# A transformer kernel's opening reordered on all engines: rope of the first half inside the second LayerNorm, keys of two heads loaded first, scores begun on half the tokens

## The reference, cut to what matters

```python
x = L0_attn_x
mod = (_silu(L0_c) @ L0_wmod).reshape(L0_c.shape[0], 6, 1, -1)
h = _layernorm(x, axis=-1) * (1 + ca) + sa
...
q = (x @ Wq.T).reshape(b, t, H, DH).transpose(0, 2, 1, 3)      # H=32, DH=16
k = (x @ Wk.T).reshape(b, t, HKV, DH).transpose(0, 2, 1, 3)    # HKV=8, G=H//HKV=4
v = (x @ Wv.T).reshape(b, t, HKV, DH).transpose(0, 2, 1, 3)
q = q * cos + _rotate_half(q) * sin
k = k * cos + _rotate_half(k) * sin
scores = jnp.einsum('bhgtd,bhkd->bhgtk', qg, k) / math.sqrt(DH)
scores = jnp.where(causal[None, None, None], scores, jnp.finfo(jnp.float32).min)
attn = jax.nn.softmax(scores, axis=-1)
ctx = jnp.einsum('bhgtk,bhkd->bhgtd', attn, v)
```

## Time and profile before

| what | value |
|---|---|
| time, median of 3 runs | 879.16 us (876.94 to 880.44) |
| the profiled execution's own time | 878.1 us |
| its span, from first to last instruction | 876.3 us |
| PE busy | 755.4 us (86%) |
| DVE busy | 521.5 us (60%) |
| ACT busy | 323.4 us (37%) |
| POOL busy | 252.7 us (29%) |
| mean granted TensorE clock | 0.93 of full speed |
| first score matmul of head 0 | at 75.42 us |
| row maxima of head 0 (`nm`) | at 108.11 us |
| first transposed unit of head 0 | at 118.64 us |

### The profile page before, as it was taken

How to read it: one execution, slowest core, us unless ns; L and a number is a source line. 1 busy time by engine, 2 the same in 40 slices (tenths; PEclk the granted TensorE clock), 3 DMA queues, 4 the chain that set the end, 5 groups by cost and what they waited for, 6 DMA issues and landing times.

```text
span 876.3 us, 11777 instructions
## 1 busy us (share of the span) xinstructions
PE 755.4 (86%) x4006; PEld 483.0 (55%) x4006; DVE 521.5 (60%) x761; ACT 323.4 (37%) x544; POOL 252.7 (29%) x190
## 2 busy tenths in 40 slices
PE   2785699999999999879799999677777799998998
PEld 1663243333333433217668888555546678886786
DVE  7733886766767677306845547898798433335410
ACT  3130035665656556661325400334412332322200
POOL 5533733200000000151236532364523122212500
PEclk9795679999999999999999999978698899999999
DMA  8084765610110100211013200110041011111111
GB/s 321 1 163 54 162 140 125 99 62 1 60 61 0 61 28 34 88 37 60 1 49 96 72 1 1 66 37 0 1 75 61 0 62 37 45 48 49 61 60 37
DMA packets 24139, 52.91 MB, mean 60 GB/s; under 512 B 3841, under 2 KB 9833, under 8 KB 22953
## 3 DMA queue, kind: packets, MB, share of 16 engines
q1 hardware_dynamic: 24105, 52.46, 22.7%
HBM read 45.63 MB, written 6.62 MB: 60 GB/s over the span
## 4 chain that ended last, share of the span: by engine, by line
PE 67%; DVE 16%; issue 5%; POOL 4%; ACT 3%; DMA 3%; SPq 1%; ACTq 0%; DVEq 0%; POOLq 0%
PE ps L830 65%; DVE mxp L1655 3%; DVE xnb L1557 1%; ACT pr L1372 1%; DVE arena L1566 1%; PE ps L847 1%; DMA wm<-in_wm 1%; DVE arena L1569 1%; DMA Qst<-q_parts 1%; DMA q_parts<-parts 1%; DVE rt L1850 1%; PE ps L992 1%; DVE st L1539 1%; POOL arena L2056 1%; SPq L702 1%
## 5 line engine op out<-in xcount | busy, mean ns | idle before, releaser
L830 PE MATMUL ps<-arena 128*128 128x512 f32 (+1 forms) x1728 | 429.3, 410 | 37.8 <-DVE arena L1569 15.1
L830 PEld LDWEIGHTS ps<-arena 128*128 128x128 f32 (+1 forms) x1728 | 336.9, 197 | 120.3 <-issue 29.0
L1655 DVE TENSOR_REDUCE mxp<-ps 128x2 f32<-128x1024 f32 (+3 forms) x160 | 173.4, 1116 | 86.4 <-PE ps L830 85.7
L1372 ACT ACTIVATE pr<-ps 128x512 f32<-128x512 f32 x288 | 161.7, 596 | 128.4 <-PE ps L830 125.9
L830 PE MATMUL ps<-Kst,Qst 96*128 (+4 forms) x384 | 107.3, 352 | 21.0 <-DMA Qst<-q_parts 13.8
L830 PE MATMUL ps<-Qst,Kst 99*128 (+1 forms) x288 | 104.7, 385 | 7.5 <-ACT pr L1372 4.3
L830 PEld LDWEIGHTS ps<-Kst,Qst 96*128 (+1 forms) x384 | 37.1, 103 | 88.4 <-issue 48.5
L830 PE MATMUL ps<-maskb,identb 128*128 128x128 bf16 (+1 forms) x320 | 77.7, 264 | 0.0
L830 PE MATMUL ps<-pr,vr 128*32 128x512 f32 x576 | 76.7, 605 | 0.7 <-ACT pr L1372 0.7
L830 PEld LDWEIGHTS ps<-Qst,Kst 99*128 (+1 forms) x288 | 27.2, 97 | 76.3 <-ACT pr L1372 50.0
L2104 POOL COPY vr<-vtok 128x128 f32 (+1 forms) x8 | 2.3, 293 | 204.1 <-PE ps L830 204.1
(11 more groups left out here) (180 smaller groups left out, 735.7 us busy)
## 6 DMA issues: line engine op xcount, KB each, us to landing
wmr<-in_wmr SPq DMA_DIRECT2D x8, 1280.0 KB, 5.5
raw<-in_w SPq DMA_DIRECT2D x16, 512.0 KB, 3.3
Qst<-q_parts SPq DMA_DIRECT2D x18, 256.0 KB, 8.8
q_parts<-qparts SPq DMA_DIRECT2D x3, 768.0 KB, 8.4
x<-in_x SPq DMA_DIRECT2D x8, 256.0 KB, 6.1
wm<-in_wm SPq DMA_DIRECT2D x1, 2048.0 KB, 8.7
raw<-in_up SPq DMA_DIRECT2D x8, 256.0 KB, 2.6
raw<-in_down SPq DMA_DIRECT2D x8, 256.0 KB, 2.6
```

What stands on the lines that cost most here:

```text
L830: return nc.tensor.matmul(outp, lhs, rhs, start=start, stop=stop, skip_group_check=True)
L1372: A(pr[:, k % PRING, :], ps[:, 4 + k % 2, :], ACT.Exp, scale=float(DH) ** -0.5).then_inc(exp_done, 1)
L1655: V.tensor_reduce(mxp[:, kh, g0:g0 + heads, i].rearrange("p (b e) -> p b e", e=per), units, AXX, ALU.max)\
```

## The change

The line numbers of the changed file differ; the names are the same.

- SP: `wm0` comes in four DMAs, one for each of its chunks, with a semaphore each; the second half of x is loaded ahead of the query weights; cosine and sine are loaded by halves. Jobs 0 and 1 are both stored before anything is read back. Of the keys only heads 0 and 1 are read back for each half (`load_keys(0, 2, ...)`), and the keys of heads 2 to 7 after all of them, for the whole length (`k_rest`). Each half has semaphores of its own.
- ACT: writes the three rows of ones of `Kst` (POOL did), splits the key and value weights between the chunks of the first LayerNorm, and takes the first part of job 0 between chunks 1 and 2 of the second.
- POOL: no memset of `Kst`; `wkv_lo` between its two low parts of half 0; the second `rstd` ahead of both `wq_lo_`; sines of jobs 0 and 1 and the last part of job 0 around and inside the second half's low parts.
- DVE: rope of job 0 ahead of the second half's split; job 1's rope and job 0's rest between chunks 1 and 2 of that split (`first_queries`); jobs 2 and 3 afterwards.
- PE: `values(0)` ahead of `queries(0, 0)`; `queries(2, 0)` ahead of the scores; the scores begin once the first half's stacks are in; `queries(2, 1)`, the turning of the values and the wait for the second half's stacks stand ahead of unit 6 (`LATER`); `queries(3, 0)` and `(3, 1)` move from behind units 3 and 6 to behind units 9 and 13. `swap_queries` on DVE moves with them: ahead of unit 6, behind unit 9, behind unit 19.

```diff
-            sp.dma_start(wm0[:, :, :].rearrange("p c n -> p (c n)"), a["wm0"]).then_inc(wm0_in, 16)
+            for kc in range(KC):
+                sp.dma_start(wm0[:, kc, :], a["wm0"][:, 1024 * kc:1024 * (kc + 1)]).then_inc(wm0_in[kc], 16)
...
+            for hf in range(2):
+                for n in (2 * hf, 2 * hf + 1):
+                    store_parts(n)
+                stored(2 * hf)
+                load_keys(0, 2, tok[hf], k_in[hf])
+                stored(2 * hf + 1)
+                load_queries(0, tok[hf], q0_in[hf])
+            load_keys(2, NKV, slice(0, T), k_rest)
...
             keys(0)
             ln_turn(0, 1)
+            values(0)
             weights(pe, ("wqkv", 1))
             queries(0, 0)
             ln_split(pe, 0, 1)
             keys(1)
             queries(0, 1)
-            for hf in range(2):
-                values(hf)
-            for hf in range(2):
-                queries(1, hf)
-            for hf in range(2):
-                values_turn(hf)
-            for hf in range(2):
-                queries(2, hf)
+            values(1)
+            queries(1, 0)
+            queries(1, 1)
+            queries(2, 0)
...
-            pe.wait_ge(k_in, 2 * 96)
-            pe.wait_ge(q_in[0], 2 * 96)
+            pe.wait_ge(k_in[0], 96)
+            pe.wait_ge(q0_in[0], 96)
             for s in range(NS):
+                if s == LATER:
+                    queries(2, 1)
+                    for hf in range(2):
+                        values_turn(hf)
+                    pe.wait_ge(k_in[1], 96)
+                    pe.wait_ge(q0_in[1], 96)
                 s_unit(0, s)
-                if s in (3, 6):
-                    queries(3, s // 6)
+                if s in (9, 13):
+                    queries(3, (9, 13).index(s))
...
+            dve.wait_ge(trig_in[0], 32)
+            rope_begin(0)
+            rope_end(0)
+
+            def first_queries():
+
+                rope_begin(1)
+                rope_rest(0)
+                rope_end(1)
+
+            ln_hi_(0, 1, first_queries)
+            rope_rest(1)
...
-            nc.gpsimd.memset(Kst[KROWS:KROWS + 3, :, :], 1.0).then_inc(kst_ones, 1)
-            pool.wait_ge(kst_ones, 1)
             rstd(0, 0)
-            wkv_lo()
-            ln_lo_(0, 0)
+            ln_lo_(0, 0, wkv_lo)
+            rstd(0, 1)
             wq_lo_(0)
+            pool.wait_ge(trig_in[0], 32)
+            sines(0)
             wq_lo_(1)
-            rstd(0, 1)
-            ln_lo_(0, 1)
```

More of the change, by code:

```diff
@@ L284 @@
 NS = len(SUNITS)
+LATER = next(s for s, (i, _, _, _) in enumerate(SUNITS) if i >= NT // 2)
 AHEAD = 6
@@ L695, in load_keys, with stored @@
+            def stored(n):
+                sp.wait_ge(part_out[n % 3], 16 * (n // 3 + 1))
+            def load_keys(n0, n1, tok_, done):
                 for r, part in enumerate(K_PARTS):
-                    sp.dma_start(Kst[DH * r:DH * (r + 1), :, tok[hf]],
-                                 kscr[part, :, tok[hf]].rearrange("(n d) t -> d n t", d=DH)).then_inc(k_in, 16)
-            def load_queries(c, tok_):
+                    sp.dma_start(Kst[DH * r:DH * (r + 1), n0:n1, tok_],
+                                 kscr[part, DH * n0:DH * n1, tok_].rearrange("(n d) t -> d n t", d=DH)).then_inc(done, 16)
@@ L1351, in _ @@
                     .then_inc(read_b[b], 1)
-            for c in (2, 3):
-                for hf in range(2):
-                    queries_out(c, hf)
+            for hf in range(2):
+                queries_out(3, hf)
             def copy_ctx(n):
@@ L1607, in first_modulation, with rope_begin, rope_end, rope_rest @@
                     .then_inc(read_b[b], 1)
+            swap = [p ^ 8 for p in range(32)]
+            def rope_begin(n):
+                job = ("q", 0, n // 2) if n % 2 else ("k", n // 2)
+                b = filled(dve, job)
+                V.stream_shuffle(rsw[:, n % 2, :], ps[:, b, :], swap).then_inc(rope_sw, 1)
+                if n >= 3:
+                    dve.wait_ge(part_l, n - 2)
+                V.tensor_tensor(rq[n % 3][:, :], ps[:, b, :], cosb[:, tok[n // 2]], ALU.mult).then_inc(read_b[b], 1)
+            def rope_end(n):
+                evacuated(dve, ("q", 0, n // 2) if n % 2 else ("k", n // 2))
+                dve.wait_ge(rope_sin, n + 1)
+                V.tensor_tensor(rq[n % 3][:, :], rq[n % 3][:, :], rsw[:, n % 2, :], ALU.add).then_inc(rope_q, 1)
+            def rope_rest(n):
+                dve.wait_ge(part_h, n + 1)
+                V.tensor_tensor(rq[n % 3][:, :], rq[n % 3][:, :], parts[n % 3][:, 0, :], ALU.subtract).then_inc(part_r, 1)
             for hf in range(2):
@@ L2035, in rstd, with ln_lo_ @@
                 nc.gpsimd.tensor_tensor(rs[:, hf, :], ve[:, :], mh[:, :], ALU.pow).then_inc(ln_rstd, 1)
-            def ln_lo_(L, hf):
+            def ln_lo_(L, hf, between=None):
                 for c in range(0, KC, 2):
+                    if c == 2 and between:
+                        between()
                     n = 8 * L + 4 * hf + c
```

181 lines of the change are left out of this document (94 added, 87 removed).

## The result

The changed kernel takes **873.11 us** (median of four runs, 872.28 to 874.11). The kernel before took 878.83 us beside it (four runs). The ratio is 0.994, with a 95% interval of 0.992 to 0.9961, so the change saves 5.7 us. The prediction was 872.4 us and 6.8 us.

A forecast was written before the change was run, and what follows sets the result against it. The opening's waits up to the first transposed unit bound the gain; PE bounds the rest. Row maxima ten us earlier, less 3.2 in a new wait, gives 6.8: 878.1 to 871.3, or 872.4 on the median's scale; range 866.5 to 877.5.

The forecast's parts named there:

- the light key loads absorb the late keys(1): Second half's stacks: key loads of 192 instead of 768 KB absorb the 9.3 us by which keys(1) start later.
- a new wait ahead of that unit: First transposed unit: ready by the scores at 108.6, waits until 111.8 for the row maxima's DMAs behind big loads; 3.2 us lost.
- no wait of the unit for those DMAs: Sign that would show the forecast wrong: the first transposed unit does not wait for the row maxima's small DMAs.
- `mod0` 2.8 us earlier: Opening: with `wm0` in four pieces, the last landing at 11.75, ACT's first chunk moves from 17.00 to 14.2.
- The memset on ACT, about 7 us, costs nothing: Opening: ACT writes the rows of ones, over by 11.3 at the latest, before its next work at 12.7.
- Keys(0) at 22.6: First half's split on POOL and DVE: keys(0) start at 22.6 instead of 24.04, 1.4 us earlier.
- Keys(1) at 47.9 after a gap of 7.4 us, then at half clock: PE, second half: keys(1) start at 47.9 instead of 38.63, after 7.4 us idle, and take 5.1 us at 1.2 GHz.
- The second half's stacks at 75.5, unit 6 at 76.3: Scores: second half's query loads are in at 75.5 (75.3 before); PE starts unit 6 at 76.3 at full clock.
- queries(3, 1) done at 89.8, row maxima at 98.1: Scores: last query product ends at 89.8 against 90.0 before; row maxima come at 98.1 instead of 108.11.
- Now they are issued at about 102.4, into the backlog: End of the opening: the row maxima's small DMAs, issued at 102.4 behind the loads of queries 1, land at 111.7.
- That unit starts about 22 us after queries(3, 1) ends: Rule offered for this kernel: the first transposed unit starts about 22 us after the last query product ends.
- The rival of the slower side: Queue does not absorb the delay of keys(1): stacks land at 84.6, 0 to 6 us slower, up to 885; chance 0.10.

The follow-up runs named there:

- The two parts taken back: Changed kernel with keys of all eight heads loaded for each half again: 878.65 us; changed kernel with no score before the second half's stacks are in: 881.97 us.

## Why the prediction was right, and where its steps were not

**The time** was right within 0.7 us. The main reasons given hold: everything is decided before the first transposed unit, the light key loads absorb the late keys(1), and part of what the scores win is lost in a new wait ahead of that unit. The two parts taken back bear this out (878.65 and 881.97 us). But the new wait was not the one named, and the closeness is partly luck. The forecast had the row maxima 10.0 us earlier and 3.2 lost again behind them, and measured were 10.3 and 5.2. That is a unit 1.7 us late (113.52 against 111.8) and a profiled execution of 873.0 us against 871.3. The 1.1 us added for the distance between profile and median brought the figure within 0.7; the changed kernel's profile lies only 0.1 under its median. In front of that, an opening 1.5 us late at keys(1) was made good in the scores: from unit 6's first maximum to `nm` it took 20.0 us, and 21.8 were forecast. One of the prediction's own signs of being wrong, no wait of the unit for those DMAs, came true in the trace, if only by 0.1 us.

- *`mod0` 2.8 us earlier:* not in this run. ACT's first chunk came at 16.84, 0.16 earlier, and not at 14.2. The step said "The bytes ahead are the same, so the last piece lands at 11.75 as before". The landing varies by 2 us between executions. The rest was forecast too short as well: from the landing to the first chunk it took 3.2 us and not 2.45. One profile, the run with all keys loaded with each half, had the last piece at 12.09 and the chunk at 14.21, just as forecast. The pieces did win 2.0 us against one piece. Most of that is gone by the row maxima, as the one-piece run shows.
- *The memset on ACT, about 7 us, costs nothing:* 7.02 us, and nothing. *Its removal from POOL wins nothing:* confirmed by the run with it back.
- *Keys(0) at 22.6:* 24.86, 2.3 late with the landing. Their twelve matmuls took 4.38 us instead of 5.49.
- *Normalising beside `wq_lo_(0)`:* 1.91 + 2.56 = 4.47 forecast, 3.80 measured; the turning starts at 32.79 instead of 31.3.
- *Keys(1) at 47.9 after a gap of 7.4 us, then at half clock:* 49.42, 6.69 us, and 0.50 in the windows until 54. The mechanism is right, and the lateness is the opening's.
- *The second half's stacks at 75.5, unit 6 at 76.3:* the loads, issued from 68.43, were in at 76.5. PE was still turning the values then, so its own work set unit 6, whose maxima start at 77.80 after 1.32 us of waiting:

```profile
77.80 4.29 DVE L1700 TENSOR_REDUCE mxp<-ps 128x2 f32<-128x1024 f32 x4 [1.32 <-PE ps L841]
...
89.84 0.36 SPq L737 DMA_DIRECT2D wmr<-in_wmr  x1
```

- *queries(3, 1) done at 89.8, row maxima at 98.1:* 89.84 and 97.81. The stalls for the two products were 0.65 and 1.63 us, not 0.9 and 2.0, at full clock.
- *Loads of queries 1 from 97.6:* 98.52.
- **The step that failed:** "Now they are issued at about 102.4, into the backlog". The row maxima's DMAs were issued at 107.06. I took DVE's work between `nm` and that issue as before, with 3.0 us for the four small operations (one of them, 2.24 us, beside POOL even then), and did not ask what POOL does at that time. POOL starts its rope of queries 2 when the store of queries 1 has landed, at 98.5. Before, that was ten microseconds ahead of `nm`, and now it is the same moment. So the four took 8.1 us. The backlog, which I named as the wait, was real but hidden behind this one: it shows in full when POOL is held back (7.95 us), and by 0.6 to 1.4 us in four other runs. The unit started at 113.52, against 111.8 forecast.
- *The backlog's own size was too small:* 3.2 us of waiting were forecast. With POOL held back the small DMAs, issued from 101.55, landed at 114.7 and not at 111.7. The loads began 1.2 us later than forecast in that run. And the 11.6 us of the earlier trace rows is the median of two loads; the later one landed at 112.4 in the kernel before, 0.7 after the 111.7 that I took. So the right port time alone would not have given the right end.
- *"That unit starts about 22 us after queries(3, 1) ends":* 23.7 here, but no rule of the kernel. With the store moved ahead of the wait for queries(3, 1) and POOL waiting, it is 20.5, and with the row DMAs first, POOL waiting and the rope behind the split 16.5 (85.28 to 101.80).
- The rival of the slower side, a delay that reaches the scores in full, needed the queue to be full. With all the keys in each load it is, and no gain is left.

The rule "One DMA, not several" of the Trainium skill, "SBUF — State Buffer", summary of rules for kernel authors, speaks against the four pieces, which the forecast priced at up to 1.4 us. The trace does not bear it out: the run in one piece is not faster (874.39 against 873.11 us, intervals 0.9935 to 0.9982 and 0.992 to 0.9961). The 512 B for line rate of the Trainium skill, "DMA: Bandwidth & Descriptors", Specifications, is not enough for the loads into the stacks: with rows of 2 KB the window from 102 to 105 us shows 132 GB/s at a full DMA share.

## What to carry to other kernels

When a change moves a stage earlier, ask of every engine what it will do at the new time, not what it did beside the stage before: here the maxima came ten microseconds earlier, just as POOL's rope began, and four operations of 0.2 to 0.3 us became 8.1 us. A wait that is removed can have another behind it of nearly the same length (the port, then the DMA queue); test them alone and together, since neither alone shortened the stretch of 15.7 us, and both together made it 8.6. A store or load that is needed early should not stand in a queue behind a wait that has nothing to do with it: moving one store ahead of such a wait took 1.0 us from that stretch, and 3.2 with POOL held back. And before a difference of a few microseconds between two profiles is called the edit's, compare a point ahead of the edit: here the openings alone differed by up to 2.5 us.

## What the runs showed that I had not expected

- Small DVE operations beside a row of POOL operations did not share the port in turns as short as themselves. Each of the four ended with one whole POOL operation (2.16, 2.45, 2.32, 1.15 us beside 2.36, 2.34, 2.34, 1.05), though DVE had the next one ready at once. Holding POOL back brought them to 0.21 and 0.28.
- The first large load landed between 11.75 and 13.9 us after the start, in different executions of kernels whose transfers up to it are the same or nearly so. A forecast of such a landing from one trace has this error.
- Three DMAs of 8 KB landed 1.9 us after their issue on an empty queue, and 5.0 to 11.8 us behind 1.5 MB of loads. How long they took went with when those loads were issued, at one and the same size.
